# Two staging buffers with ScalarE-issued copies, and one tensor_tensor for the source comparison of a scattered group

## The chip, the cores and the metric

The kernel is one program on 1 core of a Trainium2 chip. The metric is the device time of one execution in microseconds (us); the median of 3 runs stands for the kernel. TensorE (PE) multiplies, VectorE (DVE) and ScalarE (ACT) work elementwise, GpSimd (POOL) issues indirect transfers, SyncE (SP) issues plain ones, and 16 DMA engines move the data.

## The reference, cut to what matters

One layer of a graph network over 6250 nodes of 64 features and 200000 edges, sorted by destination:

```python
h = relu(layernorm(x))
row, col = src, dst                                   # dst is sorted, src is random
msg = relu(concat([h[col], edge_attr]) @ W1a + b1a) @ W1b + b1b
agg = segment_sum(msg, row, 6250) / max(count(row), 1)
out = x + relu(concat([h, agg]) @ W2a + b2a) @ W2b + b2b
```

Because `dst` is sorted, the rows read for a group of edges lie close together; because `src` is random, the sum over it is a true scatter.

## The kernel before

**The two kinds of groups.** The edges are worked in groups. A dense or *routed* group (kind `DN`, 120 of them, 8 tiles of 128 edges) has its messages sorted by destination bucket with one-hot matmuls and summed on chip. A *scattered* group (kind `S`, 101 of them, 6 tiles) has equal sources inside a tile combined by a matmul with a 0/1 matrix, and is then added to one of four tables in HBM by indirect transfers from POOL (L733).

**The loop.** `cycles` calls each engine's `cycle(s, n, t, routes, sums_too)` 126 times, with the same order on all engines. In turn `t` one group is routed (for t below 120), one S group is worked in five turns of six (`n` is 1, else 0), and from turn 6 on the group of the *macro* before is summed. A macro is six routed groups. Engines meet only at semaphores; each works through its own list in order.

**Routing, staging, skewing.** For a routed group PE makes six fills (`route`, L1678, 4 matmuls each) into two PSUM banks in turn; ACT copies each fill to SBUF (`keep_routed`, L973), into `staged`, which exists once. Fill `f` may start when the copy of fill `f-2` is done. PE puts one of the sums of the earlier macro (`sum_nodes`, L1693, 12 matmuls of 128x65) behind each fill, and six more behind the last. When the sixth fill is in `staged`, SP (`skew`, L581) issues 4 DMAs, or 7 in the last turn of a macro (27 per macro, 540 in all, counted by the semaphore `skewed`), which move the 4 strips of 32 lanes to `routed`, each shifted by its strip. The first `keep_routed` of the next turn waits until all of these have landed (`act.wait_ge(skewed, SKEWED_UP_TO[t.base])`), since it overwrites `staged`. The other reader of `skewed` is DVE: `locals_of` (L1239) of a macro needs all copies of its six groups. `routed` itself is double buffered by macro.

**The lists around it.** SP in a turn: `refill(S)` (waits for PE's z of that group, then 5 DMAs: two ids, two windows, one e_t), `refill(DN)` (3 DMAs), then `skew`. ACT in a turn: `keep_rows` (L962, waits for PE's `combine`, L1667), `split` of S (L951), the digits (L956), `split` of DN (L951), the six `keep_routed`, with two more `split` between them where the group isn't split on DVE. DVE in a turn: the second half of `nodes` (L1248, one-hots for the sums), `pick_first` (L1217, L1222), `hot` (L1181), `same_src` (L1188), `split_rows` (L1199), `hot` of DN, `split_dense` (L1210) for two groups in five, `add_sums` (L1256, waits for PE's sums), `slots` (L1231, the one-hots for the next route, which wait for the last fill), `locals_of` and the first half of `nodes` for the next turn, `add_sums`. In the first turn of a macro's sums `locals_of` and both halves of `nodes` stand behind `hot` of DN, and PE puts its sums behind the fills only from the fourth fill on.

**The source comparison.** `same_src` makes, for each of the six tiles of an S group, a 128x128 matrix of 0 and 1 in bf16: the row of int16 ids of the tile's sources (`ids_s`, broadcast to all lanes) compared with one f32 column of `srcf`. These are six `tensor_scalar`.

**Setup.** `src_t` (L936) is made from `srcf` by ACT, and DVE waits for `src_ready` at 2 before the loop. At the end of the loop SP waits for all skewed copies before it loads `x` over the place of `staged`.

Of the kernel before, what the change touches and what calls it, by code (L numbers as in the profile page):

```python
# [6 lines left out]
P = 128  # L7
# [120 lines left out]
SKEWED_UP_TO = tuple(16 * sum(len(skews(k)) for k in range(g)) for g in range(DENSE + 1))  # L128
# [55 lines left out]
def gnn_kernel(nc, x, e_t, e_rows, src_col, dst_col, src_row, dst_row, weights, row_biases, out):  # L184
# [5 lines left out]
    with ExitStack() as ctx:  # L190
# [75 lines left out]
        staged = loop_words(0, n_staged).bitcast(bf16).rearrange("p (x c) -> p x c", c=RW)  # L266
# [87 lines left out]
        ids_i = srcf[:].bitcast(i32)  # L354

# [73 lines left out]
        lane_step, bias_ready, place_step, digit_step = sems("lane_step bias_ready place_step digit_step")  # L429
# [8 lines left out]
        skewed, x_back = sems("skewed x_back")  # L438
# [48 lines left out]
        with nc.Block() as block:  # L487

            @block.sync
            def _(sp):  # L490
# [84 lines left out]
                def skew(t):  # L575

                    sp.wait_ge(routed_ready, done(t.times(len(FILLS), len(FILLS))))
                    macro = t.base // MACRO % 2
                    for q, first, last, to in skews(t.base):
                        lanes = slice(q * PLACES, (q + 1) * PLACES)  # L580
                        sp.dma_start(routed[lanes, macro, to:to + last - first, :, :].rearrange("p x b c -> p (x b c)"),  # L581
                                     staged[lanes, first * BLOCKS:last * BLOCKS, :].rearrange("p x c -> p (x c)")).then_inc(skewed, 16)
# [16 lines left out]
                sp.wait_ge(skewed, SKEWED_UP_TO[DENSE])  # L599
# [40 lines left out]
            def _(pool):  # L640
# [62 lines left out]
                nc.gpsimd.tensor_scalar(digits[:, :, :, 0], by_tile(bucket_b), -float(UNITS), None, ALU.mult).then_inc(digit_step, 1)  # L703
                nc.gpsimd.tensor_scalar(digits[:, :, :, 1], by_tile(lane), P - 1.0, 1.0, ALU.min, ALU.add).then_inc(digit_step, 1)
                pool.wait_ge(digit_step, 2)
                nc.gpsimd.tensor_tensor(digits[:, :, :, 0], digits[:, :, :, 0], by_tile(column), ALU.add).then_inc(digit_step, 1)
                nc.gpsimd.tensor_tensor(digits[:, :, :, 1], digits[:, :, :, 1], by_tile(over), ALU.add).then_inc(digit_step, 1)
# [170 lines left out]
            def _(act):  # L878
# [57 lines left out]
                nc.scalar.activation(src_t[:], srcf[:, DT:COLS], ACT.Identity, bias=untrash[:]).then_inc(src_ready, 1)  # L936
                act.wait_ge(w_in, 16)
# [5 lines left out]
                def main(fit):  # L943
# [22 lines left out]
                    def keep_routed(t, f):  # L966

                        act.wait_ge(routing, done(t.times(len(FILLS), f + 1)))
                        bank = l1_ps[f % 2][:, 0:2 * RW].rearrange("p (i c) -> p i c", c=RW)
                        if fit:  # L970
                            if f == 0 and t.base:
                                act.wait_ge(skewed, SKEWED_UP_TO[t.base])
                            nc.scalar.activation(staged[:, 2 * f:2 * f + 2, :], bank, ACT.Copy).then_inc(routed_ready, 1)  # L973
                            return
                        if f == 0:
                            act.wait_ge(dense_ended, done(t.value()))
                        mine = [i for i, (_, block) in enumerate(FILLS[f]) if block < SUB]
                        tiles = [side * SUB + block for side, block in FILLS[f] if block < SUB]
                        nc.scalar.activation(dsame[:, tiles[0]:tiles[-1] + 1, :], bank[:, mine[0]:mine[-1] + 1, :], ACT.Copy
                                             ).then_inc(routed_ready, 1)  # L980

                    def cycle(s, n, t, routes, sums_too):
# [52 lines left out]
            def _(dve):  # L1035
# [134 lines left out]
                dve.wait_ge(src_ready, 2)  # L1170
# [177 lines left out]
                def fast():  # L1348
# [57 lines left out]
                    dve.wait_ge(digit_step, 4)  # L1406
# [8 lines left out]
                def general():  # L1415
# [81 lines left out]
                    dve.wait_ge(digit_step, 4)  # L1497
                    step(nc.vector.memset(oh1[:], 0.0))
                    step(nc.vector.memset(words(0, n_routed), 0.0))
                    step(nc.vector.memset(loop_words(0, n_staged), 0.0))  # L1500
# [386 lines left out]
```

## Time and profile before

| | us |
|---|---|
| median of 3 runs | 1493.0 |
| lowest, highest | 1477.75, 1494.9 |
| the profiled execution | 1496.89 |
| its span, first to last instruction | 1495.1 |
| busy in the span: PE, DVE, POOL, ACT | 1254.7, 1298.6, 1057.6, 644.6 |

The profile is one execution. Busy is time in which an instruction of the engine runs; idle before a line is the time its engine waited, put down to what ended the wait. A DMA issue is not counted as busy time of its engine. Starts are in us from the span's start; a timeline line with x4 merges four instructions, and what stands in brackets is the wait ahead of it.

### The profile page before, as it was taken

How to read it: one execution, taken by the hardware profiler on the slowest of the kernel's cores; microseconds unless marked ns; L12 is line 12 of the kernel's file. 1: busy time of each engine (PE TensorE's matmuls, PEld its weight loads, DVE VectorE, ACT ScalarE, POOL GpSimd, SP SyncE). 2: the span in 40 equal slices, each digit the busy share in tenths (PEclk: the TensorE clock that was granted, in tenths of full speed). 3: DMA queues.
4: the chain of work that ended last, by engine and by line, in shares of the span. 5: the costliest groups of instructions: out<-in, count | busy, mean ns of one | idle time of the engine just before them, and what ended most of it. 6: DMA issues, size and time to landing. Idle time of an engine off the chain costs nothing. (4 is left out here: it accounts for less than half of the span.)

```text
span 1495.1 us, 64007 instructions
## 1 busy us (share of the span) xinstructions
PE 1254.7 (84%) x26084; PEld 1188.2 (79%) x26084; DVE 1298.6 (87%) x4459; ACT 644.6 (43%) x1429; POOL 1057.6 (71%) x702
## 2 busy tenths in 40 slices
PE   3555889889889889888889889899988989888867
PEld 3455789888888889888878779888878889888765
DVE  7886799897889889897989789899989999798787
ACT  6234444444445344444444444444534444344305
POOL 3978786775758686676868586686868668586724
PEclk9778999999999999998999999999999999899999
DMA  5769788886879798796978687787978878787552
GB/s 158 273 163 193 159 181 166 168 171 145 166 152 185 164 183 169 158 189 133 187 161 175 152 173 170 157 178 171 188 151 185 169 161 193 139 189 142 104 160 81
DMA packets 243297, 249.02 MB, mean 167 GB/s; under 512 B 151959, under 2 KB 192664, under 8 KB 241848
## 3 DMA queue, kind: packets, MB, share of 16 engines
q1 hardware_dynamic: 154744, 217.80, 53.5%
q0 software_dynamic: 88256, 27.10, 23.0%
q8 instruction: 207, 3.39, 1.0%
q14 instruction: 90, 0.74, 0.2%
HBM read 140.75 MB, written 31.76 MB: 115 GB/s over the span
## 5 line engine op out<-in xcount | busy, mean ns | idle before, releaser
L733 POOL DMA_INDIRECT sums<-vv,sidx x606 | 969.7, 1600 | 373.2 <-DVE sidx L1222 180.7
L1693 PE MATMUL rank_ps<-area,loop 128*128 128x65 bf16 x17640 | 660.6, 196 | 7.8 <-DVE loop L1248 4.7
L1693 PEld LDWEIGHTS rank_ps<-area,loop 128*128 128x128 bf16 x17640 | 636.6, 100 | 11.1 <-DVE loop L1248 5.8
L1678 PE MATMUL rank_ps<-r_d,oh 128*128 128x196 bf16 x2880 | 387.0, 262 | 165.1 <-ACT loop L973 155.7
L973 ACT ACTIVATE loop<-rank_ps 128x392 bf16<-128x392 f32 x720 | 346.4, 497 | 265.3 <-DMA area<-loop 183.3
L1248 DVE TENSOR_SCALAR loop<-iota,local 128x512 bf16<-128x512 int16 (+1 forms) x1440 | 438.5, 372 | 4.2
L1678 PEld LDWEIGHTS rank_ps<-r_d,oh 128*128 128x128 bf16 x2880 | 237.9, 101 | 209.6 <-ACT loop L973 181.9
L1231 DVE TENSOR_SCALAR oh<-iota,rank 128x384 bf16<-128x384 int16 x960 | 255.9, 337 | 15.0 <-PE rank_ps L1678 15.0
L951 ACT ACTIVATE r_d<-z_ps 128x512 f32<-128x512 f32 x258 | 154.5, 599 | 142.2 <-PE z_ps L1648 118.5
L962 ACT ACTIVATE vv<-c_ps 128x396 f32<-128x396 f32 x101 | 50.6, 501 | 282.0 <-PE c_ps L1667 276.2
L1256 DVE TENSOR_TENSOR dense<-rank_ps,dense 128x260 f32<-128x260 f32 x240 | 102.1, 426 | 74.7 <-PE rank_ps L1693 74.1
L1642 PE MATMUL z_ps<-wts,et_d 128*128 128x128 f32 x960 | 137.7, 287 | 0.9 <-ACT r_d L951 0.7
L1642 PEld LDWEIGHTS z_ps<-wts,et_d 128*128 128x128 f32 x960 | 118.1, 194 | 1.2 <-ACT r_d L951 1.0
L1199 DVE TENSOR_TENSOR r_s<-r_s 128x384 f32<-128x384 f32 x202 | 111.7, 553 | 3.5
L1188 DVE TENSOR_SCALAR loop<-ids_s,srcf 128x128 bf16<-128x128 int16 x606 | 108.4, 284 | 0.0
L1642 PE MATMUL z_ps<-wts,et_s 128*128 128x128 f32 x606 | 94.2, 293 | 0.0
L951 ACT ACTIVATE r_s<-z_ps 128x384 f32<-128x384 f32 x101 | 49.6, 491 | 73.7 <-PE z_ps L1648 70.4
L1642 PEld LDWEIGHTS z_ps<-wts,et_s 128*128 128x128 f32 x606 | 77.3, 195 | 0.0
L1239 DVE SCALAR_TENSOR_TENSOR local<-area 128x12 f32<-128x12 bf16 x120 | 20.5, 171 | 63.7 <-DMA area<-loop 63.7
L1667 PE MATMUL c_ps<-r_s,loop 128*128 128x64 bf16 (+1 forms) x1818 | 73.8, 195 | 1.5 <-issue 1.5
L1210 DVE TENSOR_TENSOR r_d<-r_d 128x512 f32<-128x512 f32 x102 | 70.0, 686 | 1.8
L1667 PEld LDWEIGHTS c_ps<-r_s,loop 128*128 128x128 bf16 x1818 | 64.5, 98 | 1.7 <-issue 1.6
(208 smaller groups left out, 848.5 us busy)
## 6 DMA issues: line engine op xcount, KB each, us to landing
area<-loop SPq DMA_DIRECT2D x420, 147.0 KB
ids_s<-ids SPq DMA_DIRECT2D x202, 192.0 KB
et_d<-in_e_t SPq DMA_DIRECT2D x120, 256.0 KB
ids_d<-ids SPq DMA_DIRECT2D x120, 256.0 KB
et_s<-in_e_t SPq DMA_DIRECT2D x101, 192.0 KB
sums<-vv,sidx POOLq DMA_INDIRECT x606
sums<-dense POOLq DMA_DIRECT2D x4, 1625.0 KB
area<-loop SPq DMA_DIRECT2D x40, 110.2 KB
```

What stands on the lines that cost most here:

```text
L733: nc.gpsimd.indirect_dma_start(out=sums[t][:, :], out_offset=bass.IndirectOffsetOnAxis(ap=index, axis=0), in_=rows, in_offset=None, comput ...
L951: nc.scalar.activation(rows3(kind, g)[:, :, PARTS[r]:PARTS[r] + D], z, ACT.Relu).then_inc(split_ready[kind], 1)
L973: nc.scalar.activation(staged[:, 2 * f:2 * f + 2, :], bank, ACT.Copy).then_inc(routed_ready, 1)
L1188: ins = nc.vector.tensor_scalar(same[:, g.mod(2), k, :], ids_s[:, g.mod(SR), 0, k * P:(k + 1) * P], srcf[:, column_of(S, g, k):column_of(S ...
L1199: nc.vector.tensor_tensor(r3[S][:, :, PARTS[r + 1]:PARTS[r + 1] + D], r3[S][:, :, at:at + D], halves(S, g)[:, :, at:at + D], ALU.subtract) ...
L1231: ins = nc.vector.tensor_scalar(oh1[:, k, :], iota[:, 0:BLOCKS * P], pos[:, bass.ds(t.value(k * DENSE), 1)], None, ALU.is_equal)
L1248: nc.vector.tensor_scalar(oh2[h][:, g, 0:units * P], iota[:, 0:units * P], local[:, n.mod(2), at:at + 1], None, ALU.is_equal).then_inc(nod ...
L1256: nc.vector.tensor_tensor(part, l2_ps[h][:, 0:width], part, ALU.add).then_inc(summed, 1)
L1642: nc.tensor.matmul(z_ps[kind][:, j * P:(j + 1) * P], et[kind][:, slot, j * P:(j + 1) * P], wts[:, C_W1A_BOT:C_W1A_BOT + P], start=j == 0, ...
L1667: t = nc.tensor.matmul(c_ps[b][:, k * R:k * R + n], same[:, b, k, :], halves(S, g)[:, k, PARTS[r]:PARTS[r] + n], start=r == 0, stop=r == 2)
L1678: ins = nc.tensor.matmul(l1_ps[f % 2][:, i * RW:(i + 1) * RW], oh1[:, k, block * P:(block + 1) * P], halves(DN, t)[:, k, :], start=k == si ...
L1693: ins = nc.tensor.matmul(l2_ps[h][:, u * W:u * W + w], oh2[h][:, g % MACRO, u * P:(u + 1) * P], rows[:, PARTS[r]:PARTS[r] + w], start=g % ...
```

## The change

- `staged` becomes a list of two buffers, used by group in turn; the second one is a new SBUF tensor.
- `skew` moves from SP's list to the end of ACT's turn: ACT waits until its sixth `keep_routed` is done and issues the 4 or 7 DMAs.
- There is a semaphore for each buffer. The first `keep_routed` of turn `t` waits for the copies of turns up to `t-2` out of its own buffer. DVE's `locals_of` waits for both.
- `same_src` is one `tensor_tensor` over six tiles (768 elements per lane). Its second operand is a copy of the source columns as int16, each value twice (`src_pairs`), written by ACT in the setup over the columns of `srcf` that `src_t` was made from; its pattern is 6 tiles, 64 repeats with step 0, 2 adjacent values. DVE waits for `src_ready` at 3.
- `digit_step` is merged into `lane_step` (counts 10 to 13), a memset of `staged` in the branch for general inputs is dropped, and SP's wait for the copies before it loads `x` becomes a wait for the first sum of turn 120.

```diff
-SKEWED_UP_TO = tuple(16 * sum(len(skews(k)) for k in range(g)) for g in range(DENSE + 1))
+def landed_copies(g, slot):
+    return 16 * sum(len(skews(k)) for k in range(slot, g, 2))
...
-        staged = loop_words(0, n_staged).bitcast(bf16).rearrange("p (x c) -> p x c", c=RW)
+        staged = [a.bitcast(bf16).rearrange("p (x c) -> p x c", c=RW) for a in (loop_words(0, n_staged), sb("staged", [P, n_staged])[:])]
...
+        src_pairs = srcf[:, DT:COLS].bitcast(i16).rearrange("p (c a) -> p c a", a=2)
...
@@ SP
-                def skew(t):
-                    sp.wait_ge(routed_ready, done(t.times(len(FILLS), len(FILLS))))
-                    macro = t.base // MACRO % 2
-                    for q, first, last, to in skews(t.base):
-                        lanes = slice(q * PLACES, (q + 1) * PLACES)
-                        sp.dma_start(routed[lanes, macro, to:to + last - first, :, :]...,
-                                     staged[lanes, first * BLOCKS:last * BLOCKS, :]...).then_inc(skewed, 16)
...
-                        skew(t)
...
-                sp.wait_ge(skewed, SKEWED_UP_TO[DENSE])
+                sp.wait_ge(summing, done(BUCKETS * (DENSE - MACRO) + 1))
...
@@ ACT
+                act.wait_ge(src_ready, 2)
+                nc.scalar.activation(src_pairs, src_t[:].rearrange("p (c a) -> p c a", a=1).to_broadcast([P, COLS - DT, 2]),
+                                     ACT.Identity, bias=trash[:]).then_inc(src_ready, 1)
...
-                            if f == 0 and t.base:
-                                act.wait_ge(skewed, SKEWED_UP_TO[t.base])
-                            nc.scalar.activation(staged[:, 2 * f:2 * f + 2, :], bank, ACT.Copy).then_inc(routed_ready, 1)
+                            if f == 0 and t.base > 1:
+                                act.wait_ge(skewed[t.mod(2)], landed_copies(t.base, t.mod(2)))
+                            nc.scalar.activation(staged[t.mod(2)][:, 2 * f:2 * f + 2, :], bank, ACT.Copy).then_inc(routed_ready, 1)
...
+                    def skew(t):
+                        act.wait_ge(routed_ready, done(t.times(len(FILLS), len(FILLS))))
+                        for q, first, last, to in skews(t.base):
+                            lanes = slice(q * PLACES, (q + 1) * PLACES)
+                            act.dma_start(routed[lanes, t.base // MACRO % 2, to:to + last - first, :, :]...,
+                                          staged[t.mod(2)][lanes, first * BLOCKS:last * BLOCKS, :]...).then_inc(skewed[t.mod(2)], 16)
...
+                            if fit:
+                                skew(t)
...
@@ DVE
-                dve.wait_ge(src_ready, 2)
+                dve.wait_ge(src_ready, 3)
...
-                    for k in range(TILES[S]):
-                        ins = nc.vector.tensor_scalar(same[:, g.mod(2), k, :], ids_s[:, g.mod(SR), 0, k * P:(k + 1) * P],
-                                                      srcf[:, column_of(S, g, k):column_of(S, g, k) + 1], None, ALU.is_equal)
-                    ins.then_inc(same_ready, 1)
+                    first = g.base * TILES[S]
+                    own = src_pairs[:, first:first + TILES[S], :].rearrange("p k (h a) -> p k h a", h=1).to_broadcast([P, TILES[S], P // 2, 2])
+                    nc.vector.tensor_tensor(same[:, g.mod(2), :, :].rearrange("p k (h a) -> p k h a", a=2),
+                                            ids_s[:, g.mod(SR), 0, :].rearrange("p (k h a) -> p k h a", k=TILES[S], a=2),
+                                            own, ALU.is_equal).then_inc(same_ready, 1)
...
-                    dve.wait_ge(skewed, SKEWED_UP_TO[(macro.base + 1) * MACRO])
+                    for slot in range(2):
+                        dve.wait_ge(skewed[slot], landed_copies((macro.base + 1) * MACRO, slot))
```

## Rows read from the trace of the kernel before

**Rows 1.** The page's first part: the span and busy time of each engine.

```profile
span 1495.1 us, 64007 instructions
PE 1254.7 (84%) x26084; PEld 1188.2 (79%) x26084; DVE 1298.6 (87%) x4459; ACT 644.6 (43%) x1429; POOL 1057.6 (71%) x702
```

**Rows 2.** Busy by window: 112 turns of the loop, then three single turns.

```profile
core 0: us, PE busy (x) PEld busy (x) DVE busy (x) ACT busy (x) POOL busy (x), PEclk, DMA share, GB/s
158.10:1396.70 1238.60, 1100.26 (x23927) 1055.67 (x23927) 1104.62 (x3917) 554.88 (x1218) 898.87 (x563) 0.96 0.81 167
1189.00:1198.40 9.40, 8.89 (x202) 8.74 (x203) 7.27 (x24) 5.40 (x12) 7.88 (x6) 1.00 0.85 182
1198.40:1209.90 11.50, 10.38 (x231) 9.79 (x228) 11.36 (x39) 4.60 (x11) 9.67 (x7) 1.00 0.91 197
```

**Rows 3.** Waits of the whole span: waiter and releaser; us in total, times, longest.

```profile
ACT vv L962 <- PE c_ps L1667: 276.2, 98, 4.5
ACT loop L973 <- DMA area<-loop: 183.3, 90, 5.0
...
POOL sums L733 <- DVE sidx L1222: 180.7, 26, 12.9
...
PE rank_ps L1678 <- ACT loop L973: 155.7, 85, 5.5
...
DVE dense L1256 <- PE rank_ps L1693: 74.1, 56, 3.7
...
DVE local L1239 <- DMA area<-loop: 63.7, 20, 4.6
```

**Rows 4.** Timeline of one turn: sixth fill, copies, first fill of the next.

```profile
796.53 1.06 ACT L973 ACTIVATE loop<-rank_ps 128x392 bf16<-128x392 f32 x2
...
797.98 3.00 SPq L581 DMA_DIRECT2D area<-loop  x4
...
800.23 0.50 ACT L962 ACTIVATE vv<-c_ps 128x396 f32<-128x396 f32 x1 [2.65 <-PE c_ps L1667]
...
804.83 0.89 ACT L973 ACTIVATE loop<-rank_ps 128x392 bf16<-128x392 f32 x2 [1.87 <-DMA area<-loop]
...
805.39 0.53 PE L1678 MATMUL rank_ps<-r_d,oh 128*128 128x196 bf16 x4 [1.39 <-ACT loop L973]
```

**Rows 5.** Timeline of the first turn of a macro's sums, behind 7 copies.

```profile
887.21 5.82 SPq L581 DMA_DIRECT2D area<-loop  x7
...
894.80 0.18 DVE L1239 SCALAR_TENSOR_TENSOR local<-area 128x12 f32<-128x12 bf16 x1 [4.11 <-DMA area<-loop]
...
895.41 1.48 PE L1678 MATMUL rank_ps<-r_d,oh 128*128 128x196 bf16 x8 [3.82 <-ACT loop L973]
```

**Rows 6.** Groups by line on DVE: count, busy us, mean ns, idle before.

```profile
L1248 DVE TENSOR_SCALAR loop<-iota,local 128x512 bf16<-128x512 int16 x1320 | 398.7, 369 | 4.2
...
L1199 DVE TENSOR_TENSOR r_s<-r_s 128x384 f32<-128x384 f32 x202 | 111.7, 553 | 3.5
L1188 DVE TENSOR_SCALAR loop<-ids_s,srcf 128x128 bf16<-128x128 int16 x606 | 108.4, 284 | 0.0
...
L1210 DVE TENSOR_TENSOR r_d<-r_d 128x512 f32<-128x512 f32 x102 | 70.0, 686 | 1.8
L1181 DVE TENSOR_SCALAR hots_d<-ids_d,basew 128x1024 bf16<-128x1024 int16 x120 | 63.7, 531 | 0.0
L1181 DVE TENSOR_SCALAR loop<-ids_s,basew 128x384 bf16<-128x384 int16 x202 | 59.8, 337 | 0.8 <-issue 0.8
```

**Rows 7.** One line at a time: duration ns min/median/max, first and last start.

```profile
L581 SPq DMA_DIRECT2D area<-loop x540: 507/592/2412, 100.3 to 1413.5; - x180
...
L1199 DVE TENSOR_TENSOR r_s<-r_s x202: 537/555/627, 85.2 to 1398.9; 128x384 f32<-128x384 f32 x101
...
L733 POOL DMA_INDIRECT sums<-vv,sidx x606: 1546/1572/2337, 89.1 to 1434.4; - x152
```

**Rows 8.** Waits of the SP queue, whole span, same columns as rows 3.

```profile
SPq L581 <- ACT loop L973: 157.0, 61, 8.4
```

More of the change, by code:

```diff
@@ L428, in gnn_kernel @@
         high_ready, mid_ready, low_ready = sems("high_ready mid_ready low_ready")
-        lane_step, bias_ready, place_step, digit_step = sems("lane_step bias_ready place_step digit_step")
+        lane_step, bias_ready, place_step = sems("lane_step bias_ready place_step")
         hot_ready, z_ready, split_ready, zsum_ready = (sems(f"{n}_s {n}_d") for n in ("hot", "z", "split", "zsum"))
@@ L437, in gnn_kernel @@
         table_done, early_in, half_in, early_added = sems("table_done early_in half_in early_added")
-        skewed, x_back = sems("skewed x_back")
+        skewed = [sem(f"skewed{slot}") for slot in range(2)]
+        x_back = sem("x_back")
         gidx_ready = sems("gidx_ready_s gidx_ready_d")
@@ L573, in _ @@
                 refill(DN, Count(0))
-                def skew(t):
-                    sp.wait_ge(routed_ready, done(t.times(len(FILLS), len(FILLS))))
-                    macro = t.base // MACRO % 2
-                    for q, first, last, to in skews(t.base):
-                        lanes = slice(q * PLACES, (q + 1) * PLACES)
-                        sp.dma_start(routed[lanes, macro, to:to + last - first, :, :].rearrange("p x b c -> p (x b c)"),
-                                     staged[lanes, first * BLOCKS:last * BLOCKS, :].rearrange("p x c -> p (x c)")).then_inc(skewed, 16)
                 def cycle(s, n, t, routes, sums_too):
@@ L702, in _ @@
                 pool.wait_ge(lane_step, 9)
[L703 to L707, printed above, removed]
+                nc.gpsimd.tensor_scalar(digits[:, :, :, 0], by_tile(bucket_b), -float(UNITS), None, ALU.mult).then_inc(lane_step, 1)
+                nc.gpsimd.tensor_scalar(digits[:, :, :, 1], by_tile(lane), P - 1.0, 1.0, ALU.min, ALU.add).then_inc(lane_step, 1)
+                pool.wait_ge(lane_step, 11)
+                nc.gpsimd.tensor_tensor(digits[:, :, :, 0], digits[:, :, :, 0], by_tile(column), ALU.add).then_inc(lane_step, 1)
+                nc.gpsimd.tensor_tensor(digits[:, :, :, 1], digits[:, :, :, 1], by_tile(over), ALU.add).then_inc(lane_step, 1)
                 pool.wait_ge(low_ready, done(NTURNS))
@@ L980, in keep_routed @@
                                              ).then_inc(routed_ready, 1)
+                    def skew(t):
+                        act.wait_ge(routed_ready, done(t.times(len(FILLS), len(FILLS))))
+                        for q, first, last, to in skews(t.base):
+                            lanes = slice(q * PLACES, (q + 1) * PLACES)
+                            act.dma_start(routed[lanes, t.base // MACRO % 2, to:to + last - first, :, :].rearrange("p x b c -> p (x b c)"),
+                                          staged[t.mod(2)][lanes, first * BLOCKS:last * BLOCKS, :].rearrange("p x c -> p (x c)")
+                                          ).then_inc(skewed[t.mod(2)], 16)
                     def cycle(s, n, t, routes, sums_too):
@@ L1405, in fast @@
                     step(nc.vector.tensor_tensor(pos, pos, place, ALU.add))
-                    dve.wait_ge(digit_step, 4)
+                    dve.wait_ge(lane_step, 13)
                     slots(Count(0))
@@ L1496, in general @@
                     dve.wait_ge(place_step, PLACED)
-                    dve.wait_ge(digit_step, 4)
+                    dve.wait_ge(lane_step, 13)
                     step(nc.vector.memset(oh1[:], 0.0))
                     step(nc.vector.memset(words(0, n_routed), 0.0))
-                    step(nc.vector.memset(loop_words(0, n_staged), 0.0))
                     step(nc.vector.memset(loop_words(first_oh2, n_oh2), 0.0))
```

## The prediction

> **What bounds the kernel now.** The page's first part comes first [rows 1]: DVE is busy for 87% of the span and PE for 84%, ACT for 43%. No engine is full, so the next view is the loop by itself [rows 2]. Its window runs from one first fill to another, 112 turns apart: 1238.6 us, so 11.06 us per turn. PE is idle in 1238.6 - 1100.3 = 138.3 us of it and DVE in 1238.6 - 1104.6 = 134.0 us, about 1.2 us per turn each. Then the waits [rows 3] say for what. PE waits 155.7 us, in 85 turns, for ACT's copy of a fill (L973). ACT waits 183.3 us ahead of that copy for the DMAs that empty `staged`. DVE waits 74.1 us for PE's sums (L1256) and 63.7 us, in 20 turns, for the same DMAs ahead of L1239. These lines name one chain, and the timeline shows it in a turn [rows 4]: the sixth fill is in `staged` at 796.53 + 1.06 = 797.59, SP issues four copies from 797.98 to 800.98, and the next first fill can be written only at 804.83, when they have landed; ACT waited 1.87 us for it and PE then 1.39 us. So 7.2 us pass from the last fill of one turn to the first of the next. That is the recurrence that the one buffer imposes, and DVE then waits for the sums that PE does late.
>
> The other half of the picture is how full the rest is. Two turns in a row took 9.40 and 11.50 us; DVE was busy for 7.27 us of the first and 11.36 us of the second [rows 2]. In turns like the second one, where DVE also splits the dense rows, DVE is the bound and no wait stands there to be removed.
>
> **The second buffer: PE's side.** The wait ahead of L973 goes, 183.3 us on ACT, since copies two turns old are long landed. Not all of PE's 155.7 us can return. In the first turn of a macro's sums [rows 5] DVE waits for the seven copies just issued, until 894.80, and needs L1239 (0.18) and a first one-hot (399 / 1320 = 0.30 us of busy time each [rows 6]) before PE can sum. PE's wait of 3.82 us there lies ahead of the third fill. After the change it passes the third and fourth fill (0.53 us each [rows 4]) and stands ahead of its first sum. 3.82 - 1.06, about 2.8 us, remain in each of 20 such turns, 56 us. PE's gain is at most 155.7 - 56 = 100 us.
>
> **The second buffer and the comparison: DVE's side.** DVE's 74.1 us for PE's sums can go; the 63.7 us stay, because the copies still start at the sixth fill. The six `tensor_scalar` cost 108.4 / 101 = 1.07 us per S group [rows 6]. The trace has no `tensor_tensor` of two-byte values, so I bound it. Upper end: the f32 `tensor_tensor` of 384 and 512 elements, 553 and 686 ns, rise by 1.04 ns per element, so 768 cost 553 + 384 x 1.04 = 952 ns, a gain of 0.12 us per group, 12 us in all. Lower end: the two-byte `tensor_scalar` of 384 and 1024 elements, 337 and 531 ns, rise by 0.30 ns, so 337 + 384 x 0.30 = 453 ns, a gain of 0.62, 62 us in all. By operation the first is nearer, by type the second; I take the middle, 0.70 us, a gain of 0.37 x 101 = 37 us. DVE's gain is at most 74 + 37 = 111 us.
>
> By a page the middle is a little dear. The Trainium skill, "Vector Engine (DVE) Microarchitecture Reference", section "Performance modes", says that two sources of two bytes run two elements per cycle, also where a row is read again and again with step 0. With the 0.96 GHz and some 150 fixed cycles of "VectorE: DVE Perf Modes", an estimate from these pages is (384 + 150) / 0.96 = 556 ns, and the gain would be 52 us instead of 37. No row here shows it.
>
> **What ACT takes over.** 540 DMA issues move from SP to the end of ACT's turn, 4.5 per turn, with a wait for its own sixth copy ahead of them. No DMA is issued by ACT in this trace; the nearest rows are SP's issues of the same copies, 507/592/2412 ns [rows 7], 0.75 us each in [rows 4] and 0.83 in [rows 5]. I take 0.75: four cost 3.0 us. Behind them on ACT is `keep_rows` (L962), which now waits for PE's `combine` for 276.2 us in 98 turns, 2.8 us each [rows 3], 2.65 in the turn shown [rows 4]. That wait covers the issues but for about 0.3 us. What is late then is L962 and the splits behind it; the chain that PE needs is the first fill, which moves from 804.83 to soon after the split of DN, so 0.3 us of delay uses up part of a slack and costs nothing on PE. With seven issues ACT is 3 us late, in the turn in which PE stands still for DVE anyway. At the lower end (0.51) the cover is whole; the upper end (2.41) is the slower rival below. Were the cover gone, 3.0 us in each of 120 turns would be 360 us. SP loses the same issues: in 59 of 120 turns it came to them later than the sixth fill (it waited for ACT in 61 [rows 8]), 0.39 us later in [rows 4]. The copies start that much earlier. Nothing is queued behind them on SP that waits, so no gain is booked.
>
> **The rest.** `src_pairs` is one ACT instruction of 1212 elements per lane in the setup; from the 1.06 us of two fills of 392 elements [rows 4] some 1.6 us, once, behind `src_t`; even on the path it would be 1.6 us, and `same_src`, its reader, stands behind DVE's ranks: nothing. Merged semaphores and the memset in the other branch: nothing. SP's wait for the copies becomes one for the first sum of turn 120, which itself needs the copies; the load of `x` behind it is wanted two turns later: nothing, and some 10 us, a turn, if it were late by one. POOL waits 180.7 us for indices [rows 3], so it has room for a loop shortened by 100 us.
>
> **The sum.** The smaller of 100 and 111 us is the ceiling. Of it I keep two thirds, 67 us: DVE-bound turns such as the 11.50 us one shorten only by the 0.37 of the comparison, and PE and DVE, each with about 1.2 us idle per turn, have to be late in different turns without waiting for each other. The span falls from 1495.1 to 1428 us. The profiled execution (1496.89) is 3.9 us above the median 1493.0, so the predicted median is 1493 - 67 = 1426 us. A difference of 2% is about what a measurement of this kernel can tell from none: below 1463 is faster, above 1523 slower.
>
> **The rivals.**
> - *Only part comes back* (0.20). PE's wait moves from L973 to the one-hots of DVE (L1231, L1248), since turns bound by DVE set the pace, or to DMAs that land later, because the 16 engines are busy for 0.81 of the loop already [rows 2]. For: DVE at 11.36 of 11.50. Against: DVE waited 74.1 us for PE, in 56 turns. What stays is the comparison and little else, 20 to 40 us: 1463 us.
> - *More comes back* (0.13). The copies start up to a microsecond earlier and SP's later loads no longer mix with them, so that the first turns gain too, and the comparison costs 0.45. Then the gain is the 111 of DVE's side or a little more: 1378 us. Against: the landing time in [rows 5] is made of issues one after the other, which stay.
> - *The comparison collides with POOL* (0.03). The new instruction has two inputs in SBUF, beside POOL's scatters of 1.57 us each [rows 7]. If it waited 0.6 us on average it would cost 1.3 us, 0.23 more than the six: DVE's side falls to 74 - 23 = 51 us, of which two thirds are 34: 1459 us. Against: L1199, with two SBUF inputs too, spreads only from 537 to 627 ns [rows 7]. The Trainium skill, "SBUF — State Buffer", section "Who interferes with whom", has the rule: a DVE instruction with two SBUF inputs contends with a GpSimd one that reads SBUF, and the later one blocks. The trace so far shows at most 0.09 us of that.
> - *ACT becomes the bound, slower than before* (0.07). ACT is busy 554.88 / 112 = 4.95 us per turn [rows 2], and an issue holds its list. The turn is 11.06 us, so it decides from (11.06 - 4.95) / 4.5 = 1.36 us per issue. At 1.5 us a turn takes 4.95 + 6.75 = 11.7 us: 0.64 x 120 = 77 us more, 1570 us. For: single issues on SP took up to 2.41 us. Against: their median is 0.59.
>
> **How the numbers follow.** The forecast has 0.57, with its own range 1393 to 1450: the comparison at either end moves DVE's side to 86 or 136, and half of the lower ceiling is 43, all of PE's 100. The range 1382 to 1475 adds the most of the first two rivals and the third, and leaves out the slower one and the ends. Faster by over 2%: 0.57, 0.13, 0.02 and a fourth of the first rival's 0.20, together 0.77; slower 0.07; the rest, 0.16, within 2%.
>
> **What would show it.** The wait of L973 for DMAs near zero, and that of L1678 for L973 below 20 us; a new wait of L1693 for L1248 of some 50 us, at the 20 first turns; L1256's wait for PE below 30 us; L1239's wait for DMAs still about 60; L1188's successor at 0.55 to 0.95 us; ACT's issues at 0.5 to 0.9 us each and L962's idle time gone. The prediction is wrong if ACT's issues take over a microsecond, if L1678 waits for L1231 instead, or if PE and DVE both stay at 1.2 us idle per turn.

## The result, and the profile after

| | before | changed |
|---|---|---|
| median, same chip | 1488.16 | 1412.89 |
| lowest, highest of 4 runs | 1477.75, 1494.9 | 1410.96, 1415.22 |
| profiled execution, span | 1496.89, 1495.1 | 1410.96, 1409.1 |

The changed kernel takes 0.9501 of the time [0.9435, 0.9566], 75 us less. The prediction was 67 us less (1426 us) and a range of 1382 to 1475: direction, main mechanism and size held, with a gain somewhat above the forecast. The profiled spans differ by 86.0 us, since the profiled execution of before (1496.89) was slower than all four timed ones and that of the changed kernel was the fastest of its four; sums over the trace below are made against this 86.

The first part of the page of the changed kernel (busy us, share of the span, instructions) and two lines of its third part (queue: packets, MB, share of 16 engines):

```profile
span 1409.1 us, 63622 instructions
...
PE 1238.7 (88%) x26084; PEld 1175.0 (83%) x26084; DVE 1255.6 (89%) x3954; ACT 644.2 (46%) x1430; POOL 1071.0 (76%) x702
...
q1 hardware_dynamic: 128824, 145.51, 39.2%
...
q10 hardware_dynamic: 25920, 72.29, 18.3%
```

DVE's busy time fell by 43.0 us against [rows 1], less than the 52.9 of the comparison below, since the one-hots L1258 (L1248 before) take 9.4 us more (447.9 us for 1440 instead of 438.5). PE's fell by 16.0. The 540 copies, 72.29 MB, now stand on a queue of their own, q10, which the page of before does not list.

The same 112 turns as in [rows 2], first fill to first fill:

```profile
146.33:1308.95 1162.62, 1085.79 (x23900) 1043.78 (x23901) 1063.25 (x3445) 555.21 (x1220) 915.60 (x567) 0.97 0.87 178
```

1162.62 / 112 = 10.38 us per turn instead of 11.06, 76.0 us in all. PE's idle time in the window fell from 138.3 to 1162.62 - 1085.79 = 76.8 us, that is by 61.5; the other 14.5 are busy time of PE (the mean granted clock rose from 0.96 to 0.97). By DVE's account the same 76.0 are 34.6 of idle time (134.0 to 99.4) and 41.4 of busy time. The remaining 86.0 - 76.0 = 10 us are the six turns ahead of the window: its start moved from 158.06 to 146.33, by 11.7, and what follows its end is 1.8 longer.

The waits of the changed kernel (what waited, for whom: us in all, times, longest):

```profile
ACT vv L959 <- PE c_ps L1676: 271.0, 88, 5.1
...
DVE local L1249 <- DMA area<-staged: 69.8, 20, 5.9
...
PE rank_ps L1702 <- DVE loop L1258: 40.0, 20, 4.7
...
DVE dense L1266 <- PE rank_ps L1702: 31.0, 29, 2.4
...
PE rank_ps L1687 <- ACT loop L970: 10.4, 13, 1.9
...
PE z_ps L1664 <- ACT r_d L948: 10.4, 8, 2.8
...
PE rank_ps L1687 <- ACT staged L970: 8.6, 5, 7.0
```

Against [rows 3]: no wait of ACT's fill copy (L973 before, L970 now) for a DMA stands in the answer any more (183.3 us before). PE's wait for that copy fell from 155.7 to 10.4 + 8.6 = 19.0 us. DVE's wait for PE's sums fell from 74.1 to 31.0. DVE's wait for the copies, in 20 turns, is still there with 69.8 (63.7 before), and behind it is a new wait of PE for DVE's one-hots, 40.0 us in 20 turns.

The answer by line and form for the new comparison, and its durations (min/median/max):

```profile
L1197 DVE TENSOR_TENSOR loop<-ids_s,srcf 128x768 bf16<-128x768 int16 x101 | 55.5, 549 | 0.0
...
L1197 DVE TENSOR_TENSOR loop<-ids_s,srcf x101: 537/551/558, 82.7 to 1302.4; 128x768 bf16<-128x768 int16 x101
```

0.549 us stand where six `tensor_scalar` took 1.07 [rows 6]: 108.4 - 55.5 = 52.9 us of DVE's time.

An ordinary turn, to be held against [rows 4] (start, us, engine, line, operation; in brackets the idle time before):

```profile
790.71 0.55 DVE L1197 TENSOR_TENSOR loop<-ids_s,srcf 128x768 bf16<-128x768 int16 x1
...
792.97 2.45 ACTq L984 DMA_DIRECT2D area<-staged  x4
...
795.52 0.50 ACT L959 ACTIVATE vv<-c_ps 128x396 f32<-128x396 f32 x1 [2.58 <-PE c_ps L1676]
...
798.14 1.06 ACT L970 ACTIVATE loop<-rank_ps 128x392 bf16<-128x392 f32 x2
```

The sixth fill ends at 792.95, ACT issues its four copies until 795.42, and L959 starts 0.1 us later. The next first fill (into the other buffer, which the trace names `loop`) is written at 798.14 with no wait for a DMA. From sixth fill to first fill are 5.2 us, where [rows 4] had 7.2.

The first turn of a macro's sums, to be held against [rows 5]:

```profile
768.99 5.55 ACTq L984 DMA_DIRECT2D area<-staged  x7
...
772.77 0.33 SPq L525 DMA_DIRECT2D ids_d<-ids  x1
...
774.59 0.22 ACT L953 ACTIVATE r_d<-rank 128x16 f32<-128x16 bf16 x1 [5.62 <-issue]
...
777.87 0.18 DVE L1249 SCALAR_TENSOR_TENSOR local<-area 128x12 f32<-128x12 bf16 x1 [3.62 <-DMA area<-staged]
...
778.50 0.84 PE L1702 MATMUL rank_ps<-area,loop 128*128 128x65 bf16 x12 [1.28 <-DVE loop L1258]
```

ACT is held for 5.62 us by its seven issues, and the last copy lands 777.87 - 774.54 = 3.3 us after its issue ended. SP loads the next dense group meanwhile.

What this comes to by turn, worked out from the starts of the first fills' copies on the timelines, and from PE's instructions between them: mean us by place in the macro, over the 18 whole macros from the window's start on. `locals_of` waits for the seven copies of a macro's last turn:

| | turn with seven copies | turn behind it | the four others, each | six turns |
|---|---|---|---|---|
| before, length | 11.57 | 11.24 | 10.91 | 66.5 |
| changed, length | 10.41 | 13.45 | 9.60 | 62.3 |
| before, PE idle | 3.16 | 0.55 | 0.96 | 7.6 |
| changed, PE idle | 1.52 | 2.11 | 0.12 | 4.1 |

Before, the wait for the seven copies stood ahead of the next first fill and so ended the turn that issued them. In the changed kernel the first fill passes it, and it lies in the turn behind. So only the two turns together can be compared: 22.81 us became 23.86, a loss of 1.05. PE's idle time in them is nearly the same (3.71 and 3.63), and its busy time grew from 19.10 to 20.23. The four others gained 1.31 us each, 5.2 per macro: 0.84 of idle time and 0.47 of PE's busy time. The difference is 4.2 us per macro, 4.2 x 18 = 76 us in the window.

### The profile page after: what moved, and what is told of

Its sections match the earlier page's. It is cut to its first block and busy times, and to the rows that moved or that the text cites. A ratio compares the mean times of both kernels' runs of the same rounds, so it can differ in the third digit from the quotient of the medians.

```text
span 1409.1 us, 63622 instructions
## 1 busy us (share of the span) xinstructions
PE 1238.7 (88%) x26084; PEld 1175.0 (83%) x26084; DVE 1255.6 (89%) x3954; ACT 644.2 (46%) x1430; POOL 1071.0 (76%) x702
## 3 DMA queue, kind: packets, MB, share of 16 engines
q10 hardware_dynamic: 25920, 72.29, 18.3%
## 5 line engine op out<-in xcount | busy, mean ns | idle before, releaser
L727 POOL DMA_INDIRECT sums<-vv,sidx x606 | 983.2, 1622 | 276.0 <-issue 167.0
L1258 DVE TENSOR_SCALAR loop<-iota,local 128x512 bf16<-128x512 int16 (+1 forms) x1440 | 447.9, 379 | 4.2
L1687 PE MATMUL rank_ps<-r_d,oh 128*128 128x196 bf16 x2880 | 374.0, 255 | 46.3 <-issue 21.5
L1687 PEld LDWEIGHTS rank_ps<-r_d,oh 128*128 128x128 bf16 x2880 | 233.9, 99 | 80.1 <-issue 25.8
L970 ACT ACTIVATE loop<-rank_ps 128x392 bf16<-128x392 f32 x360 | 174.0, 497 | 67.7 <-PE rank_ps L1687 59.6
L970 ACT ACTIVATE staged<-rank_ps 128x392 bf16<-128x392 f32 x360 | 177.6, 496 | 40.1 <-PE rank_ps L1687 30.6
L959 ACT ACTIVATE vv<-c_ps 128x396 f32<-128x396 f32 x101 | 50.5, 500 | 318.0 <-PE c_ps L1676 271.0
L948 ACT ACTIVATE r_d<-z_ps 128x512 f32<-128x512 f32 x258 | 153.8, 596 | 92.0 <-PE z_ps L1657 53.6
L1249 DVE SCALAR_TENSOR_TENSOR local<-area 128x12 f32<-128x12 bf16 x120 | 20.7, 173 | 69.8 <-DMA area<-staged 69.8
L948 ACT ACTIVATE r_s<-z_ps 128x384 f32<-128x384 f32 x101 | 49.4, 489 | 60.6 <-PE z_ps L1657 59.7
L953 ACT ACTIVATE r_d<-rank 128x16 f32<-128x16 bf16 x119 | 25.3, 213 | 99.9 <-issue 71.9
```

The lines of the kernel that those rows point to most:

```text
L727: nc.gpsimd.indirect_dma_start(out=sums[t][:, :], out_offset=bass.IndirectOffsetOnAxis(ap=index, axis=0), in_=rows, in_offset=None, comput ...
L948: nc.scalar.activation(rows3(kind, g)[:, :, PARTS[r]:PARTS[r] + D], z, ACT.Relu).then_inc(split_ready[kind], 1)
L970: nc.scalar.activation(staged[t.mod(2)][:, 2 * f:2 * f + 2, :], bank, ACT.Copy).then_inc(routed_ready, 1)
L1258: nc.vector.tensor_scalar(oh2[h][:, g, 0:units * P], iota[:, 0:units * P], local[:, n.mod(2), at:at + 1], None, ALU.is_equal).then_inc(nod ...
L1687: ins = nc.tensor.matmul(l1_ps[f % 2][:, i * RW:(i + 1) * RW], oh1[:, k, block * P:(block + 1) * P], halves(DN, t)[:, k, :], start=k == si ...
```

## The experiments

Ratios are to the kernel before on the same chip. The theory was: the one buffer's recurrence cost PE 1.2 us a turn; the second buffer gives that back, wherever the copies are issued; the comparison alone gives little since DVE's spare time then goes into a wait; what remains is the landing of the seven copies.

### One part alone

**The staging without the comparison.** The changed kernel with the six `tensor_scalar` of before:

```diff
-                    nc.vector.tensor_tensor(same[...6 tiles...], ids_s[...], own, ALU.is_equal)
+                    for k in range(TILES[S]):
+                        ins = nc.vector.tensor_scalar(same[:, g.mod(2), k, :], ids_s[...], srcf[...], None, ALU.is_equal)
```

> The changed kernel with the old comparison: six tensor_scalar per scattered group again, the second buffer and the copies issued by ACT stay. Theory (the one-buffer chain was the bound): most of the gain stays, 45 to 65 us below the kernel before, about 1430 us; the comparison at 0.55 instead of 1.07 us is then worth the remaining 10 to 30 us, and DVE's wait for PE's sums is smaller than in the changed kernel because DVE is later. Rival (DVE was the bound, the comparison carries the gain): less than 25 us below the kernel before, above 1463 us.

Measured: 1435.9 us, ratio 0.9637 [0.9587, 0.9688]. Its waits: L1239's successor 58.2 us in 20 turns, PE for one-hots 34.1, DVE for sums 26.1. The staging is worth 3.6%, about 54 us, and the comparison on top of it 0.9637 - 0.9501 = 1.4%, about 20 us. The second figure compares ratios from two chips; a pair on one chip, at the end of this section, gives 21 us.

**The comparison without the staging.** The kernel before with the new `same_src` and its `src_pairs`:

> The kernel before with the new comparison alone: one buffer, copies issued by SP. Theory: DVE's 0.52 us per scattered group turn mostly into a longer wait for PE's sums, since the chain through the one buffer is untouched; 0 to 20 us below the kernel before, 1468 to 1488 us. Rival (DVE was the bound): 40 to 52 us below, about 1442 us.

Measured: 1494.2 us, ratio 1.0015 [0.9975, 1.0056]. Its waits:

```profile
ACT loop L977 <- DMA area<-loop: 173.9, 90, 5.8
...
PE rank_ps L1683 <- ACT loop L977: 151.7, 86, 6.3
...
DVE dense L1261 <- PE rank_ps L1698: 101.0, 75, 3.9
```

DVE has 53 us less to do and none of it reaches the end. The recurrence stands as before (151.7 of 155.7), and DVE waits 101.0 us for PE's sums instead of 74.1. So the two parts are not additive: the comparison is worth nothing while the one buffer sets the pace, and about 20 us once it doesn't.

### Who issues the copies

**Two buffers, SP issues.** The changed kernel with `skew` back in SP's list behind `refill(DN)`:

```diff
@@ SP
+                def skew(t):
+                    sp.wait_ge(routed_ready, done(t.times(len(FILLS), len(FILLS))))
+                    ... sp.dma_start(routed[...], staged[t.mod(2)][...]).then_inc(skewed[t.mod(2)], 16)
...
@@ ACT
-                            if fit:
-                                skew(t)
```

> The changed kernel, but SP issues the copies at the end of its turn, as before; two buffers and the new comparison stay. Theory (the buffer matters, not who issues): within 15 us of the changed kernel, 1405 to 1428 us; DVE's wait ahead of locals_of grows a little, because SP comes to the seven copies late in some turns. Rival (the gain comes from taking the issues off SP's list, so that copies start earlier): above 1445 us.

Measured: 1424.0 us, ratio 0.958 [0.9512, 0.9647]. The interval overlaps that of the changed kernel, so with two buffers the issuing engine decides little; the buffer is the cause. In its first turn of a macro's sums:

```profile
770.74 5.34 SPq L584 DMA_DIRECT2D area<-staged  x7
776.20 0.51 SPq L525 DMA_DIRECT2D ids_d<-ids  x1
...
778.34 0.18 DVE L1248 SCALAR_TENSOR_TENSOR local<-area 128x12 f32<-128x12 bf16 x1 [4.12 <-DMA area<-staged]
```

The loads of the next group stand behind the copies here, and the last copy lands 778.34 - 776.08 = 2.3 us after its issue ended. As means over the 20 turns, from the timelines: 2.1 us with SP and 3.5 with ACT. But SP comes to the seven copies 2.0 us later, so that from the end of the sixth fill to the start of `locals_of` it is 9.1 us with SP and 8.6 with ACT (7.3 before). The pair of turns around the wait takes 24.2 us (23.9 in the changed kernel), the four others 9.63 each (9.60).

**One buffer, ACT issues.** The other half of the same cut:

```diff
-                            if f == 0 and t.base > 1:
-                                act.wait_ge(skewed[t.mod(2)], landed_copies(t.base, t.mod(2)))
-                            nc.scalar.activation(staged[t.mod(2)][...], bank, ACT.Copy)
+                            if f == 0:
+                                for slot in range(2):
+                                    if landed_copies(t.base, slot):
+                                        act.wait_ge(skewed[slot], landed_copies(t.base, slot))
+                            nc.scalar.activation(staged[0][...], bank, ACT.Copy)
```

> The changed kernel with one staging buffer: ACT issues the copies and waits, ahead of the first fill of the next turn, until all have landed, as the kernel before did; the new comparison stays. Theory: the wait of L973's successor for DMAs is back near 180 us and PE's behind it near 150; 5 to 30 us below the kernel before, 1458 to 1483 us. Rival (who issues matters): within 15 us of the changed kernel, about 1415 us.

Measured: 1551.7 us, ratio 1.0435 [1.0349, 1.0521], slower than before, which the expectation missed. Its waits:

```profile
PE rank_ps L1689 <- ACT loop L972: 179.1, 83, 5.7
...
ACT loop L972 <- DMA area<-loop: 175.2, 90, 4.1
...
DVE dense L1268 <- PE rank_ps L1704: 133.8, 80, 4.6
...
DVE local L1251 <- DMA area<-loop: 97.9, 20, 5.8
```

The recurrence is back, and longer in one place. The nearest twin is the comparison alone, also with one buffer but with SP issuing, at 1494.2 us: 57 us lie between the two. By the timelines a macro takes 69.6 us here and 66.3 there. In the turns with four copies ACT issues 0.3 us earlier after the sixth fill, and the next first fill starts 4.0 us after the last issue ends (3.5 there). So from the sixth fill to the next first it is about 6.7 us in both. In the turn with seven copies the next first fill starts 3.8 us after the last issue (2.1 there), 8.9 us after the sixth fill (7.2 there), and that turn takes 13.2 us instead of 11.5. This is 1.7 of the 3.3 us per macro. The other 1.6 are spread over five turns, and no run says what they are made of. So moving the issues to ACT by itself costs; with the second buffer the next first fill no longer waits for the landing.

### What the issues cost ACT

**Eight issues instead of four.** Each of the four copies of a turn is split into two of 16 lanes; turns with seven copies are left alone, and the bytes are the same:

```diff
+                            for half in range(halves_of):
+                                n = PLACES // halves_of
+                                lanes = slice(q * PLACES + half * n, q * PLACES + (half + 1) * n)
```

> The changed kernel, but each of the four copies of the turns that are not last in a macro is issued as two of 16 lanes: 8 issues instead of 4 in 100 turns, the same bytes. ACT's list is then held 4.9 instead of 2.5 us behind its sixth copy, 2 us more than its wait for combine covers. Theory (by the threshold of the prediction, 1.36 us per copy; here 1.2): the slack behind keep_rows takes up part of it, 0 to 60 us above the changed kernel, 1415 to 1475 us, with PE waiting for ACT again. Rival (ACT has room to spare): within 6 us, 1407 to 1419 us. Rival (an issue held on ACT is paid in full): 200 us and more above.

Measured: 1544.7 us, ratio 1.0303 [1.024, 1.0366]. The changed kernel was not timed on this chip; by its ratio it would take 0.9501 x 1505.6 = 1430 us there (1439 by its ratio of 0.9557 on a third chip, below), so the split costs 106 to 115 us. The expectation had 0 to 60, its second rival 200 and more. Its waits and one turn:

```profile
ACT vv L959 <- issue: 456.0, 78, 7.5
...
DVE dense L1269 <- PE rank_ps L1705: 118.7, 97, 4.7
...
PE z_ps L1667 <- ACT r_d L948: 73.2, 59, 2.4
```

```profile
802.82 5.16 ACTq L987 DMA_DIRECT2D area<-loop  x8
808.08 0.50 ACT L959 ACTIVATE vv<-c_ps 128x396 f32<-128x396 f32 x1 [5.29 <-issue]
```

An issue costs the same (513/611 ns minimum and median), there are twice as many, and ACT comes to L959 5.3 us after the sixth fill instead of 2.6. The wait of L959 is now mostly for the issues, and PE waits for ACT's splits (L948: 73.2 us) and fill copies (L970: 42.8 + 37.4 us). The four ordinary turns take 11.1 us each instead of 9.6, while the turn with seven copies, which are not split, stays at 9.9. ACT's busy time per turn is unchanged at about 5: what bounds is the list in its order, issues, then L959, the splits, the digits and six fill copies paced by PE.

### The landing of the seven copies

Two remedies, each aimed at one part of the wait in the 20 turns.

**Issues shared in the last turn of a macro.** SP issues 4 of the 7 copies, ACT 3:

```diff
@@ SP, skew
+                        if not (t.base % MACRO == MACRO - 1 and q > 1):
+                            continue
@@ ACT, skew
+                            if t.base % MACRO == MACRO - 1 and q > 1:
+                                continue
```

> The changed kernel, but in the last turn of each macro SP issues four of the seven copies (strips 2 and 3) and ACT three, so that the issues take about 2.5 instead of 5 us. Theory (what is left of the first turns' wait is the seven issues one after the other): DVE's wait ahead of locals_of falls from 69.8 to 20 to 45 us, PE's wait for the one-hots from 40 to under 20, the time falls by 20 to 45 us, to 1370 to 1393 us. Rival (the landing is set by the DMA engines, not by the issues): within 8 us of the changed kernel, 1405 to 1420 us.

Measured: 1384.1 us, ratio 0.9205 [0.9142, 0.9269]. Two of its waits:

```profile
DVE local L1264 <- DMA area<-staged: 41.7, 19, 4.7
...
PE rank_ps L1717 <- DVE loop L1273: 27.7, 16, 4.4
```

The seven issues span 3.5 us on average instead of 5.04, and from the sixth fill to `locals_of` it is 7.1 us instead of 8.6. PE's wait for one-hots was expected under 20 us and is 27.7. The pair of turns around the wait takes 21.8 us instead of 23.9.

**Loads held back.** SP waits, once per macro, until all copies have landed before it loads the next dense group:

```diff
@@ SP, cycle, ahead of refill(DN)
+                        if t.base and t.base % MACRO == 0:
+                            for slot in range(2):
+                                sp.wait_ge(skewed[slot], landed_copies(t.base, slot))
```

> The changed kernel, but SP waits until all copies of a macro have landed before it issues the loads of the next turn's dense refill. It tells why copies issued by ACT land 3.5 us after their last issue and those issued by SP 2.0. Theory (they share the DMA engines with loads that SP issues meanwhile, which behind SP's own copies would have stood in line): the seven copies land 2.0 to 2.6 us after the last issue, DVE's wait falls by about 20 us, the time by 10 to 25 us, to 1388 to 1403 us. Rival (a DMA issued by ACT is slower by itself): still about 3.5 us, and no gain, 1408 to 1425 us, since the loads come later.

Measured: 1386.1 us, ratio 0.9239 [0.9172, 0.9306]. DVE's wait for the copies is 48.1 us instead of 69.8. One first turn:

```profile
756.11 5.34 ACTq L987 DMA_DIRECT2D area<-staged  x7
...
763.63 0.33 SPq L525 DMA_DIRECT2D ids_d<-ids  x1
763.65 0.18 DVE L1252 SCALAR_TENSOR_TENSOR local<-area 128x12 f32<-128x12 bf16 x1 [0.94 <-DMA area<-staged]
```

With nothing loaded meanwhile, the seven copies land 763.65 - 761.45 = 2.2 us after the last issue, 2.5 on average over the 20 turns instead of 3.5, and the pair of turns takes 21.9 us. Only the loads of one dense group, three DMAs per macro, were moved. So 1.0 of the 1.4 us that a landing takes longer with ACT issuing comes from loads of SP's queue that run beside the copies; the other 0.4 is not explained. Neither remedy ran beside the changed kernel itself; on their chip the kernel with step 0 innermost (below), which is close to it, takes 1424.8 us, 39 to 41 more than they do.

### The comparison's operand

**Step 0 innermost.** The pair of adjacent equal values replaced by one value read 128 times:

```diff
-                    own = src_pairs[:, first:first + TILES[S], :].rearrange("p k (h a) -> p k h a", h=1).to_broadcast([P, TILES[S], P // 2, 2])
+                    own = src_pairs[:, first:first + TILES[S], :][:, :, 0:1].to_broadcast([P, TILES[S], P])
```

> The changed kernel with the second operand of the comparison read one value at a time (innermost step 0, 128 repeats) instead of in adjacent pairs. Theory: the instruction takes about 0.95 us instead of 0.55, which is what six tensor_scalar took, so the time is that of the changed kernel with the old comparison: 15 to 30 us above the changed kernel, 1428 to 1443 us. Rival (the pairs are not what makes it fast): 0.55 us and no difference, about 1413 us.

Measured: 1424.8 us, ratio 0.9493 [0.9426, 0.956], on a chip where the changed kernel was not timed. The ratio is that of the changed kernel, where 1 to 2% more was expected. The instruction:

```profile
L1197 DVE TENSOR_TENSOR loop<-ids_s,srcf 128x768 bf16<-128x768 int16 x101 | 95.6, 947 | 0.0
```

The pairs are what makes it fast: 947 ns without them, 549 with. What these 0.40 us per group are worth is read from the next runs, which have both on one chip.

### One chip for the last four

> The changed kernel itself, as the reference for the three runs beside it on this chip: about 0.95 of the kernel before.

> The comparison read one value at a time again (0.95 instead of 0.55 us), beside the changed kernel on the same chip, since the ratios of the two from different chips, 0.9493 and 0.9501, left open what 0.4 us on DVE is worth. Theory (outside the first turns DVE and PE are both nearly full): 10 to 30 us slower than the changed kernel. Rival (PE alone bounds those turns): within 6 us of it.

> The changed kernel with both remedies for the first turns: SP issues four of the seven last copies, and holds its next loads until they have landed. Theory: the last issue falls at about 3 us and the landing 2 to 2.5 us behind it, so DVE's wait falls to 15 to 35 us and the time to 40 to 60 us below the changed kernel, 0.91 of the kernel before. Rival (either remedy already takes all there is, because PE or DVE is next): no more than 5 us below the better of the two, 0.92 of the kernel before.

> As e9_both, with the six tensor_scalar back. Theory (DVE is the fuller engine once the first turns are short): the comparison is worth 25 to 50 us here, more than in the changed kernel. Rival (PE bounds): under 15 us.

| | median (lowest, highest) | ratio to before |
|---|---|---|
| changed kernel again | 1413.7 (1412.5, 1427.0) | 0.9557 [0.9444, 0.967] |
| step 0 innermost again | 1421.4 (1414.9, 1424.3) | 0.9589 [0.9495, 0.9682] |
| both remedies | 1373.3 (1366.4, 1377.0) | 0.9258 [0.9161, 0.9355] |
| both remedies, six `tensor_scalar` | 1394.5 (1391.8, 1404.8) | 0.9418 [0.9312, 0.9524] |

The kernel before scattered more here (1470 to 1505), so these four are better read against each other. Step 0 costs 7.6 us for 40 us of DVE time, between the two expectations and within the spread of either kernel (1412.5 to 1427.0 and 1414.9 to 1424.3), so it is not told from nothing. Both remedies together gain 40 us on the changed kernel and beat it without overlap. The new comparison is worth 21 us on top of them, of 53 us of DVE time that it frees: between what theory and rival expected. The waits of the version with both remedies:

```profile
DVE local L1267 <- DMA area<-staged: 33.8, 18, 3.5
...
PE rank_ps L1720 <- DVE loop L1276: 23.9, 16, 4.5
...
DVE dense L1284 <- PE rank_ps L1720: 19.1, 22, 2.6
```

The wait for the copies is half of the 69.8 and the wait of PE behind it 23.9 instead of 40.0. Its macro takes 60.5 us, 21.5 in the pair around the wait and 9.74 in each of the others, against 61.1 with the issues shared alone and 60.9 with the loads held back alone. Whether both are better than one is not settled by the ratios (0.9205, 0.9239, 0.9258, intervals overlapping); the turns of one execution each say 0.4 to 0.6 us per macro, about 10 us in all.

## Why the prediction was right, and where not

- **The recurrence as the cause**: right. With one buffer (comparison only) the waits and the time stay; with two, whoever issues, the time falls. L1678's wait for L973 was to fall below 20 us and is 19.0; L973's own for DMAs is gone.
- **PE's side, at most 100 us, 56 us left in the first turns**: the wait was foreseen at the right place and with the right count, 20 turns ahead of the first sum; it measures 40.0 us by the waits, 2.0 each, not 2.8. But more was left around it than the step has. PE's idle time in the pair of turns stayed at 3.6 us (3.7 before), 73 us over 20 macros. In the turn behind the copies 0.9 us of it is PE's wait for fill copies and splits of ACT, which starts 5.6 us late behind its seven issues; with SP issuing this is 0.1, and the wait for the one-hots 1.0 longer. The step "ACT is 3 us late, in the turn in which PE stands still anyway" put it at nothing and was too kind. It also counts on the wait for `combine` as cover, and that turn has no S group and no such wait: on the timeline above no L959 stands between the seven issues and L953. Sharing the issues made the pair 2.1 us shorter.
- **What no step of the prediction has**: PE's busy time. In the pair it grew by 1.1 us, so that the pair as a whole is 1.05 longer; in each of the four others it fell by 0.47. The granted clock went the same way, from 0.87 to 0.85 in the turn behind the copies and from 0.98 to 1.00 in the four others, but no run shows how much of it the clock is.
- **Two thirds of 100 kept**: 67 predicted, 75 measured, and the closeness is partly luck. By the profiled executions, which are 86 apart: the four ordinary turns gave back 1.31 us each, 105 us over 20 macros, of which 67 are idle time and the rest PE's busy time; the pair took 21 back. The reason given for the discount, PE and DVE late in different turns, is not what happened: in the ordinary turns PE's idle time fell to 0.12 us and DVE's to 0.2. What kept the gain in idle time below the ceiling lay in the pair, where the step had PE's idle time fall from about 74 to 56 us and it stayed at 73.
- **The comparison**: a mis-sized term. 0.70 us was taken, 0.549 measured, so 53 us of DVE time instead of 37, inside the bounds of 0.45 and 0.95. By the Trainium skill, "Vector Engine (DVE) Microarchitecture Reference", section "Performance modes", and "VectorE: DVE Perf Modes", the estimate was 556 ns, and the run with step 0 innermost (947 ns) agrees with its condition that the innermost dimension have step 1. Here the page was nearer than the middle of two rows. The upper bound, 952 ns from the f32 rows, is close to what the same instruction costs without the pairs.
- **What the comparison is worth in the end**: the text gave it as a part of DVE's side and not alone. Alone it is 0, with the staging 20 us.
- **ACT's issues, 0.75 each, hidden behind L962's wait**: right for four, at 2.45 / 4 = 0.61 in the turn shown and 0.65 in the mean of all 540. L959 starts 0.1 us after them there. "L962's idle time gone" was a misreading: an issue is not counted as busy, so the idle time still stands there with 271.0 us, though part of the issues lies in it.
- **The threshold of 1.36 us per issue** for the slower rival: wrong. The split copies cost 5.16 us in the turn shown, 1.29 per copy, and already lose over 100 us against the changed kernel. The formula weighed ACT's busy time against the turn, and left out the waits on PE that stand inside ACT's list. From [rows 3] the cover was 2.8 us; the second 2.6 us of issues lie outside it, and that was the figure to use.
- **"The copies start earlier, no gain booked"**: no gain came, for a reason not seen. The seven copies start 0.25 us earlier than before, but land 3.5 us after their last issue instead of 2.0, so that `locals_of` starts 8.6 us after the sixth fill instead of 7.3. Against SP with two buffers they start 2.0 us earlier and land 1.4 later.
- **POOL's collision** did not show: 537/551/558 ns over 101 instructions with no idle time ahead of them, though 99 of them run beside one of POOL's scatters. The Trainium skill, "SBUF — State Buffer", section "Who interferes with whom", has a DVE instruction with two SBUF inputs contend with a GpSimd one that reads SBUF; no duration here shows it.
- **The rest**: L1256's wait 31.0 (below 30 was foreseen), L1239's 69.8 (about 60), ACT's issues 0.61 (0.5 to 0.9). The rival "more comes back, first turns included" did not happen in the changed kernel; the two remedies reach 1373 us, near its 1378, but by another way than its sum, which came from DVE's side.

## What to carry to other kernels

A buffer that is filled, drained by DMA and filled again puts the DMA's whole landing time between two turns; a second buffer took nearly all of PE's idle time out of the ordinary turns here, and only then did a shorter list beside it pay. Price a DMA issue that moves to a compute engine as time of that engine's list, against the wait that covers it there, not against its busy share. After such a change look at the one turn in which the data is really wanted: here sharing its seven issues, or keeping the next loads out of its way for some 2 us, was worth 27 to 29 us by the medians, beside the 75 of the change. And when a wait moves across the mark that divides the turns, compare the turns on both sides of it together.

## What the runs showed of the hardware

- **The landing of a copy depends on what another queue does meanwhile.** Seven copies landed 2.1 us after their last issue on SP's queue with SP's loads behind them, 3.5 on ACT's (q10) with SP's loads running beside them, and 2.5 on ACT's with those loads held back. The Trainium skill, "DMA: Bandwidth & Descriptors", section "Issuing engines are not separate DMA queues", says that all run on the same 16 engines and interleave, and that a second issuer saves only time on the sequencer; the traces agree with the first, since holding SP's loads back changes when ACT's copies land, and here the saving on the sequencer came with 1.4 us of landing.
- **A DMA issue holds ACT's list for 514/612 ns** (minimum, median), close to SP's 507/592 [rows 7], with single ones of 2.1 us.
- **PE's clock falls around the wait**, in both kernels. In the changed one (columns: us, busy of PE, PEld, DVE, ACT, POOL, clock, DMA share, GB/s):

```profile
774.00:776.00 2.00, 0.93 (x7) 0.39 (x5) 0.24 (x1) 1.42 (x5) 1.70 (x2) 0.93 0.90 164
776.00:778.00 2.00, 1.22 (x8) 0.76 (x6) 0.13 (x1) 1.54 (x4) 1.70 (x2) 0.50 0.95 221
778.00:780.00 2.00, 1.50 (x16) 1.20 (x17) 1.97 (x8) 0.20 (x1) 1.69 (x2) 0.50 0.32 17
780.00:782.00 2.00, 2.00 (x28) 1.90 (x27) 1.84 (x6) 1.13 (x3) 1.67 (x2) 0.50 0.30 17
```

The granted clock goes to 0.50, the 1.2 GHz level, after PE has stood for part of 774 to 778, and twelve matmuls of 128x65 take 0.84 us there instead of the 0.53 at 788.62, at full clock. Over the 20 places, the slice of 2 us that begins 2 us after `locals_of` starts has a mean clock of 0.64 before and 0.60 in the changed kernel, so the fall itself is not what is new there; with both remedies it is 0.82. No run separated what the clock alone gives.
